# Row sums of a pairwise ranking on ScalarE, four buffers for the normalised rows and a loop over four batches

## The reference

```python
gt = xf.mean(axis=1) @ W_gt
kproj = xf @ W_k
score = jnp.einsum('bc,bnc->bn', gt, kproj) * SCALE
probs = jax.nn.softmax(score, axis=-1)
order = jnp.argsort(-probs, axis=-1)
reserve = order[:, :KEEP_NUM]          # KEEP_NUM = 1568 of 3136
...
```

## Time and profile before

| | us |
|---|---|
| median of 3 runs | 12256.19 (12219.48 to 12288.64) |
| profiled execution | 12231.48 |
| its span, first to last instruction | 12229.6 |
| VectorE busy | 9274.5 (76%) |
| TensorE busy | 8209.9 (67%) |
| ScalarE busy | 6990.4 (57%) |
| GpSimd busy | 2163.8 (18%) |

### The profile page before, as it was taken

How to read it: one execution, slowest core, us unless ns; L and a number is a source line. 1 busy time by engine, 2 the same in 40 slices (tenths; PEclk the granted TensorE clock), 3 DMA queues, 4 the chain that set the end, 5 groups by cost and what they waited for, 6 DMA issues and landing times. The chain is left out here.

```text
span 12229.6 us, 166452 instructions
## 1 busy us (share of the span) xinstructions
PE 8209.9 (67%) x45521; PEld 5308.0 (43%) x45521; DVE 9274.5 (76%) x26006; ACT 6990.4 (57%) x11527; POOL 2163.8 (18%) x1960
## 2 busy tenths in 40 slices
PE   4555577776575764767777677776576757344799
PEld 4555455554243432434444344443343434243587
DVE  8999544443898888989989889998889989655243
ACT  0000022112797975979999799997797979322222
POOL 2333211111000000000000000000000000077676
PEclk9999955555566655656666666665566666555555
DMA  3222100000000000000000000000000000143221
GB/s 90 71 76 63 31 22 19 20 19 21 11 17 12 18 11 12 16 12 17 17 15 18 14 14 18 18 14 14 15 14 14 18 12 15 29 96 85 54 58 40
DMA packets 669888, 351.94 MB, mean 29 GB/s; under 512 B 587281, under 2 KB 605680, under 8 KB 665056
## 3 DMA queue, kind: packets, MB, share of 16 engines
q1 hardware_dynamic: 607920, 242.84, 9.2%
q0 software_dynamic: 58624, 60.72, 1.9%
q10 hardware_dynamic: 2384, 37.11, 0.9%
HBM read 200.20 MB, written 147.72 MB: 28 GB/s over the span
## 5 line engine op out<-in xcount | busy, mean ns | idle before, releaser
L1040 PE MATMUL a_psT<-a_qt,a_kt 74*122 74x366 bf16 x3456 | 1556.8, 450 | 800.0 <-ACT a_pT L1120 558.5
L1270 DVE TENSOR_SCALAR_CACHE_REDUCE a_s<-a_psS 122x512 f32<-122x512 f32 (+1 forms) x2304 | 1605.3, 728 | 445.9 <-PE a_psS L1023 310.2
L1128 ACT ACTIVATE a_junk<-a_s,a_aim 122x1097 bf16<-122x1097 f32 x1152 | 1384.9, 1210 | 825.5 <-DVE a_s L1270 822.7
L1120 ACT ACTIVATE a_pT<-a_psT 122x732 f32<-122x732 f32 (+1 forms) x1920 | 1372.1, 715 | 598.3 <-PE a_psT L1043 594.4
L1204 DVE MAX8 a_near<-a_below 122x8 f32<-122x274 f32 (+1 forms) x4608 | 1699.3, 430 | 0.1
L1043 PEld LDWEIGHTS a_psT<-a_weigh,a_drops 122*122 122x122 bf16 x10368 | 1573.4, 191 | 193.0
L1197 DVE SCALAR_TENSOR_TENSOR a_below<-a_s,a_te,a_signs 122x1097 f32<-122x1097 f32 x1152 | 1546.4, 1352 | 128.7 <-remote 127.9
L1043 PE MATMUL a_psT<-a_weigh,a_drops 122*122 122x122 bf16 x10368 | 1527.9, 274 | 0.0
L1056 PE MATMUL a_psO<-a_pT,a_v 122*32 122x366 f32 x6912 | 1415.3, 704 | 0.0
L1128 ACT ACTIVATE a_signs<-a_s,a_te 122x1097 bf16<-122x1097 f32 x1152 | 1401.4, 1219 | 4.4 <-DVE a_te L1189 4.4
L1128 ACT ACTIVATE a_junk<-a_s,a_te 122x1097 bf16<-122x1097 f32 x1152 | 1385.1, 1205 | 0.0
(11 more groups left out here) (348 smaller groups left out, 14305.7 us busy)
## 6 DMA issues: line engine op xcount, KB each, us to landing
xbuf<-r_blank ACTq DMA_DIRECT2D x16, 1990.6 KB
e_xg<-xbuf SPq DMA_DIRECT2D x56, 568.8 KB
r_bc<-pr SPq DMA_DIRECT2D x16, 1372.0 KB, 7.4
a_k<-kT SPq DMA_DIRECT2D x384, 51.5 KB
a_q<-qT SPq DMA_DIRECT2D x384, 51.5 KB
a_kt<-kT SPq DMA_DIRECT2D x384, 51.5 KB
a_qt<-qT SPq DMA_DIRECT2D x384, 51.5 KB
r_xt<-in_x SPq DMA_DIRECT2D x16, 784.0 KB
```

The costliest lines, as they stand in the source:

```text
L1040: pe.matmul(out[:, x, 0:CW], kt[q][:, u * QP:(u + 1) * QP], qt[q][:, c * CW:(c + 1) * CW], start=True, stop=False)
L1120: act.activation(pT[j % RING][:, 0:w, :], psT[(q + j) % 2][:, 0:w, 0:CW], ACT.Exp).then_inc(exped, 1)
L1128: act.activation(out[:, :], s_[:, t, :], ACT.Sign, bias=at[:, t:t + 1], scale=-1.0, accum_out=total[:, t:t + 1]).then_inc(counted[r], 1)
L1270: dve.tensor_scalar(sc[o][:, t, a:b], psS[0:QP, a:b], 1.0, None, ALU.mult, ALU.max, accum_out=peaks[:, i, t:t + 1]).then_inc(evacuated, 1)
```

## The change

The row sums of rows 0 to 26 move to ScalarE. VectorE's comparison becomes a plain `tensor_scalar` without accumulator; ScalarE reads the bf16 marks, copies them into a throw-away tile `spill` and accumulates the row sum into the same `cnt[:, 1, j]`. A new semaphore `row_counted` frees the mark tiles together with `added`, so VectorE waits for both from row 4 on, and at the end of the batch for all 27. The last row keeps the old form. ScalarE's square and root for the next batch now stand between its copies, behind rows 1 and 6, and the clearing DMA at the start of the batch. `xls` and `idxs` get four buffers, the loop is written out for four batches per turn (four outside, a loop of two turns, four outside), and the parts move to later rows. Seventeen semaphores of `rank` are cleared at the start of `merge` on SyncE, ahead of its first loads.

```diff
-BEHIND = [0, 1, 8, 10, 11, 12, 13, 14, 15, 16]
+BEHIND = [0, 5, 10, 12, 13, 14, 15, 16, 17, 18]
+LAPS = 4
...
-        xls = [sb(f"r_xl{u}", [TP, NT, C + 1]) for u in range(2)]
+        xls = [sb(f"r_xl{u}", [TP, NT, C + 1]) for u in range(LAPS)]
...
-        idxs = [sb(f"r_idx{u}", [TP, NT], U32) for u in range(2)]
+        idxs = [sb(f"r_idx{u}", [TP, NT], U32) for u in range(LAPS)]
...
+        spill = [sb(f"r_spill{i}", [TP, N], BF16) for i in range(2)]
...
         def batches(eng, body):
 
-            for u in range(2):
-                body(0, u, True, u == 0 or B > 2)
-            if B > 4:
-                with eng.Fori(1, B // 2 - 1) as i:
-                    for u in range(2):
+            for u in range(LAPS):
+                body(0, u, True, True)
+            if B > 2 * LAPS:
+                with eng.Fori(1, B // LAPS - 1) as i:
+                    for u in range(LAPS):
                         body(i, u, False, True)
-            if B > 2:
-                for u in range(2):
-                    body(B // 2 - 1, u, False, u == 0)
+            for u in range(LAPS):
+                body(B // LAPS - 1, u, False, u < LAPS - 1)
 
...
-            with act.Fori(0, B) as b:
+
+            def square(b):
                 act.wait_ge(centred, b + 1)
                 act.activation(sq[:, :, :], xc[:, :, :], ACT.Square).then_inc(squared, 1)
+
+            def deviate(b):
                 act.wait_ge(varied, b + 1)
                 act.activation(sd, ve, ACT.Sqrt).then_inc(rooted, 1)
+
+            def body(i, u, first, more):
+                b = LAPS * i + u
                 act.dma_start(d.xbuf[bass.ds(b * TP * CLEAR, TP * CLEAR), :].rearrange("(p r) c -> p (r c)", p=TP),
                               blank[:, :, :].rearrange("p r c -> p (r c)")).then_inc(cleared, 16)
+                for j in range(NT - 1):
+                    act.wait_ge(compared, (NT - 1) * b + j + 1)
+                    if j >= 2 or not first or u:
+                        act.wait_ge(row_counted, (NT - 1) * b + j - 1)
+                    act.activation(spill[(u + j) % 2][:, j * TP:N], greater[j % MARKS][:, j * TP:N], ACT.Copy,
+                                   accum_out=cnt[:, 1, j:j + 1]).then_inc(row_counted, 1)
+                    if more and j == BEHIND[0] + 1:
+                        square(b + 1)
+                    if more and j == BEHIND[1] + 1:
+                        deviate(b + 1)
+
+            square(0)
+            deviate(0)
+            batches(act, body)
...
                 dve.wait_ge(prob_in, 16 * b + 16)
                 for j in range(NT):
                     at, to = j * TP, (j + 1) * TP
                     if j >= MARKS:
                         dve.wait_ge(added, (NT - 1) * b + j - MARKS + 1)
-
-                    more_ = dve.tensor_scalar(greater[j % MARKS][:, at:N], bc[:, at:N], rk[:, j:j + 1], None, ALU.is_gt,
-                                              ALU.add, accum_out=cnt[:, 1, j:j + 1])
+                        dve.wait_ge(row_counted, (NT - 1) * b + j - MARKS + 1)
+
                     if j < NT - 1:
-                        more_.then_inc(compared, 1)
+                        dve.tensor_scalar(greater[j % MARKS][:, at:N], bc[:, at:N], rk[:, j:j + 1], None,
+                                          ALU.is_gt).then_inc(compared, 1)
                     else:
-                        link.after(more_, 1)
+                        link.after(dve.tensor_scalar(greater[j % MARKS][:, at:N], bc[:, at:N], rk[:, j:j + 1], None, ALU.is_gt,
+                                                     ALU.add, accum_out=cnt[:, 1, j:j + 1]), 1)
                     link.after(dve.scalar_tensor_tensor(out=junk[j % 2][:, :], in0=bc[:, at:to], scalar=rk[:, j:j + 1],
                                                         in1=k.lower[:, :], op0=ALU.is_equal, op1=ALU.mult,
                                                         accum_out=cnt[:, 2, j:j + 1]), 1)
                     if more and j in BEHIND:
-                        if j == BEHIND[2] and not (first and u == 0):
-                            dve.wait_ge(scattered[1 - u], 16 * NT * (i + u))
-                            dve.wait_ge(laid[1 - u], 16 * (i + u))
-                        parts[BEHIND.index(j)](b + 1, 1 - u)
+                        v = (u + 1) % LAPS
+                        if j == BEHIND[2] and not (first and v):
+                            dve.wait_ge(scattered[v], 16 * NT * (i if v else i + 1))
+                            dve.wait_ge(laid[v], 16 * (i if v else i + 1))
+                        parts[BEHIND.index(j)](b + 1, v)
                 link.all()
                 dve.wait_ge(compared, (NT - 1) * (b + 1))
                 dve.wait_ge(added, (NT - 1) * (b + 1))
+                dve.wait_ge(row_counted, (NT - 1) * (b + 1))
...
+            for used in k.used:
+                sp.sem_clear(used)
             rows(0)
```

More of the change, by code:

```diff
@@ L229, in rank @@
          maxed, max_turned, max_one, max_all, sum_one, sum_all, probbed, prob_turned, prob_out,
-         prob_stored, prob_in, indexed, compared, added, taken, started, blanked, cleared) = (sem("r_" + x) for x in (
+         prob_stored, prob_in, indexed, compared, added, taken, started, blanked, cleared, row_counted) = (sem("r_" + x) for x in (
              "x_in", "centred", "squared", "varied", "rooted", "normed", "summed", "meaned", "gated",
@@ L233, in rank @@
              "probbed", "prob_turned", "prob_out", "prob_stored", "prob_in", "indexed",
-             "compared", "added", "taken", "started", "blanked", "cleared"))
-        scattered, laid = ([sem(f"r_{x}{u}") for u in range(2)] for x in ("scattered", "laid"))
+             "compared", "added", "taken", "started", "blanked", "cleared", "row_counted"))
+        scattered, laid = ([sem(f"r_{x}{u}") for u in range(LAPS)] for x in ("scattered", "laid"))
+        k.used = (*scattered, *laid, x_in, centred, squared, varied, rooted, normed, summed, meaned, gated, gtb_made)
         block = ctx.enter_context(nc.Block())
         def batches(eng, body):
-            for u in range(2):
-                body(0, u, True, u == 0 or B > 2)
-            if B > 4:
-                with eng.Fori(1, B // 2 - 1) as i:
-                    for u in range(2):
+            for u in range(LAPS):
[3 more added lines that the diff above has]
+                    for u in range(LAPS):
                         body(i, u, False, True)
-            if B > 2:
-                for u in range(2):
-                    body(B // 2 - 1, u, False, u == 0)
+            for u in range(LAPS):
+                body(B // LAPS - 1, u, False, u < LAPS - 1)
         def tokens(b):
@@ L267, in body @@
                 row = d.pr[bass.ds(b * NT, NT), :].rearrange("(a j) p -> a (j p)", a=1)
-                sp.dma_start(bcs[u][:, :], row.partition_broadcast(TP)).then_inc(prob_in, 16)
+                sp.dma_start(bcs[u % 2][:, :], row.partition_broadcast(TP)).then_inc(prob_in, 16)
                 sp.dma_start(d.y[bass.ds(b * N, N), :].rearrange("(j p) c -> p j c", p=TP), xls[u][:, :, 0:C]).then_inc(laid[u], 16)
             batches(sp, body)
-            for u in range(2):
-                sp.wait_ge(laid[u], 16 * (B // 2))
+            for u in range(LAPS):
+                sp.wait_ge(laid[u], 16 * (B // LAPS))
         @block.scalar
@@ L340, in body @@
                     if more and j in BEHIND[2:2 + len(parts)]:
-                        parts[BEHIND.index(j) - 2](b + 1, 1 - u)
+                        parts[BEHIND.index(j) - 2](b + 1, (u + 1) % LAPS)
             pe.wait_ge(started, 2)
@@ L356, in body @@
             def body(i, u, first, more):
-                pool.wait_ge(indexed, 2 * i + u + 1)
+                pool.wait_ge(indexed, LAPS * i + u + 1)
                 apart(pool, k)
@@ L364, in _ @@
             batches(pool, body)
-            for u in range(2):
-                pool.wait_ge(scattered[u], 16 * NT * (B // 2))
+            for u in range(LAPS):
+                pool.wait_ge(scattered[u], 16 * NT * (B // LAPS))
         @block.vector
@@ L444, in body @@
             def body(i, u, first, more):
-                b = 2 * i + u
-                bc, rk, idx = bcs[u], rks[u], idxs[u]
+                b = LAPS * i + u
+                bc, rk, idx = bcs[u % 2], rks[u % 2], idxs[u]
                 dve.wait_ge(prob_in, 16 * b + 16)
```

8 lines of the change are left out of this document (4 added, 4 removed).

## The result

The changed kernel takes 11967.17 us (median of 4 runs, 11962.35 to 11994.79) against 12248.78 us (4 runs, 12219.48 to 12288.64): ratio 0.9776, 95% interval 0.9759 to 0.9793. The prediction said 11,965. Its profiled execution has a span of 11960.6 us where the kernel before had 12229.6.

What follows compares the result with a forecast made beforehand. VectorE was taken to bound the ranking. Per batch 55.2 + 6.6 + 2.9 + 1.2 + 0.4 = 66.3 us (66.0 with overlap) gave 1042 against 1324.8, net -277 with end costs: forecast 11,965 us, range 11,900 to 12,040.

Steps and rivals of the forecast that it cites:

- What bounds the kernel: Ranking: VectorE sets the pace, busy 1216 of 1324.8 us; plain comparisons gain 23.2 us a batch.
- rival 1: Ranking comparisons: no fast reading, they keep their slope; only buffer and loop waits go, about 12,200 us; chance 4%.
- Row sums on ScalarE: Ranking: ScalarE needs 50.4 us a batch, no steady bound, but its lag makes VectorE wait 2.9 us a batch.
- rival 4: Ranking: ScalarE is the bound, with 0.7 us fixed per copy in place of 0.28; period 72, total 12,060 us; chance 8%.
- the walk: Row-by-row timing of a ranking batch with four tile buffers: VectorE waits 2.9 us, for rows 6, 7 and 8.
- two table loads of 1.28: ScalarE in each ranking batch: two loads of activation functions, 1.28 us each, within its 50.4 us.
- The parts, moved apart: Next batch's parts in the ranking: VectorE's waits for TensorE grow from 2.6 to 6.6 us a batch.
- The probabilities' way: Ranking: the probabilities' 8.9 us through memory to the broadcast is no longer fully hidden, costing 1.2 us a batch.
- Buffers and loop: Ranking: four buffers remove 25.1 us of scatter waits, fewer loop turns 12.8 us; clearing semaphores costs 1 us.
- The shared port: Ranking: fast comparisons hold GpSimd's scatters to 1.5 us in the mean, 50 us a batch; VectorE loses 0.4 us.
- rivals 2 and 3: GpSimd bounds the ranking from 2.06 us a scatter, about 12,120, 8%; or starves, slower over 2.8 us, about 12,750, 4%.
- rival 5: Ranking: TensorE's granted clock falls from 1.00 to half, bounding the period at 85; 12,240 us; chance 2%.

Runs made afterwards that it cites:

- replanning: Changed kernel with six mark tiles, VectorE's parts at other rows and TensorE's parts earlier in its queue: 11848.41 us, ratio 0.9676.
- old places: Changed kernel with the next batch's parts behind the rows that the kernel before had: 12003.21 us, ratio 0.9797.
- loop and buffers alone: Kernel before with only four buffers and the loop over four batches, sums still on VectorE: 12218.49 us, ratio 0.9976.
- control: Changed kernel without an edit, timed again beside three other kernels: 11953.10 us, ratio 0.9767.
- forms the sums twice: Changed kernel with VectorE's comparison accumulating again into an unread tile, ScalarE's copies kept: 12210.83 us, ratio 0.9966.

## Why the prediction was right, and where it was not

**What bounds the kernel; rival 1.** Right. The prediction read VectorE as the pace of the ranking; it lost 22.7 us of work a batch (363.1 / 16) where 23.2 were summed from the earlier trace rows. The plain form's slope held: 1.84 us from start to start at 2800 elements, in the batch that begins at 893, against 0.40 + 0.524 x 2.8 = 1.87. With the accumulator put back, 272 us returned, so the first rival (no fast reading) falls by an experiment and not by reading alone. The sum can be held against one batch, from 893.05, period 64.3: 0.66 us of waits at the tiles, 6.28 for TensorE's links (3.60, 1.82, 0.40, 0.46), 0.37 at the count's sum and 1.43 for the broadcast leave 55.6 for VectorE's own, as the sum had it (55.2 + 0.4). Three readings of the rows were loose: the durations of the earlier trace rows give 1.047 ns an element and not 1.042, 24 pairs in 2.37 us are 0.099 us each and not 0.096, and the 2.6 us of waits a batch count the first batch's 6.3 into the mean (2.25 without). None moves the sum by more than 0.4 us a batch.

**Row sums on ScalarE; rival 4.** The mechanism was right and two of its sizes were off. The wait costs 0.6 us a batch, not 2.9, and falls at row 10 (0.66 us ahead of the comparison at 917.95) where the walk had rows 6 to 8; the last batch alone waits 6.6. The fixed cost of a copy came out at 0.19 us from start to start (586.27 to 588.79 is 2.52 us at 2800 elements, of which 2.33 by 0.833 ns), where the prediction took 0.28 from an activation with pointer operands. "ScalarE: Activation LUTs" of the Trainium skill (§ What ACT_TABLE_LOAD costs) gives 186 ns for immediate operands; the trace agrees, with 2521 ns for a copy of 2800 elements, 189 ns over 0.833 ns an element. The larger miss is the term "two table loads of 1.28": I carried over as if a load belonged to the function, where it belongs to a change of functions as the program was built. The trace after has one load of each ahead of sixteen squares and roots, with copies between. Put back, the loads cost 22.8 us of the ranking's 27 us of error (period 64.2 and not 66.0, fifteen times), and the wait at the tiles is then 1.9 us a batch, where the walk had 2.3 with 0.19 us fixed. The same page of the Trainium skill (§ Table sets: the hidden batching unit) says that functions come in sets and that only a change of set costs; the trace after agrees, with 1 + 1 loads for 16 + 16 activations: behind the first root's load, fifteen squares, fifteen roots and all copies ran without another. The trace of before shows a program that paid although square and root can share one.

**The parts, moved apart.** Right to a few tenths: 3.6 us for the sums (predicted 3.7), 1.7 for the gate (2.0), 0.5 for the one behind (0.9 for two). Both experiments on the order took away what the prediction had named as its cause: the two rows of marks ahead of the gate (-45 us, the links behind the gate included), and the rows too few ahead of the sums (with the rest of the replanning and six tiles, -77).

**The probabilities' way.** 1.4 us a batch for 1.2, and 3.7 ahead of one batch, the one before the loop turns.

**Buffers and loop.** The buffers are necessary, which the prediction had missed: it credited them with 25.1 us, and with two of them the changed kernel is where the kernel before is (0.9982). The sum took the waits that they remove from today's periods; at the new pace a batch's scatters go on for some 50 us from its end (28 x 1.81), and the next normalisation is reached some 28 us after it (26.4 us behind the first comparison). The measured wait was 20.8; beside a VectorE that waits the 28 scatters took 46 to 48 us. At the loop's turn VectorE stood 5.6 us instead of 3.4. With the old places, where no broadcast is waited for, it stood 3.5, so the rest is perhaps the wait for the broadcast, put down to "issue", which no run shows. The 7.3 us put down to "issue" at line 502 belonged to the wait for the scatters, which fits the 48.5 us of loop and buffers alone. For the last scatters and the semaphores the sum had 6 us, and the gap behind the ranking grew by 4.3.

**The shared port; rivals 2 and 3.** Right, and the closest size of all: 1.506 us for 1.5, 50.6 us a batch. GpSimd still waits some 13 us a batch for the indices (of the 288.9 us, 104.6 stand ahead of the first scatter) and nobody waits for a scatter. The rivals needed 2.06 and 2.8 us. The point of rival 3 was whether GpSimd can take the port between two instructions that follow at once. The scatter of 579.73 did, at the end of the comparison: it was released 0.12 us behind it. The section "Who interferes with whom" of "SBUF — State Buffer" in the Trainium skill says that whoever comes second is fully blocked; this case agrees for the duration of one instruction, and its 1.506 us show that GpSimd doesn't starve beyond it.

**The clock; rival 5.** The granted clock stayed at 1.00 in the ranking's windows, TensorE busy 46 of 64 us.

**The sum.** The ranking is 305.7 us shorter where the sum had 277, and the spans differ by 269.0. The later stages gave back 36.7: 17.6 between and 19.1 at the end. The control gave back 22.7 between and took 3.1 at the end, so the end is accident; the some 20 us between stand in both executions of the changed kernel against one of the kernel before, and loop and buffers alone show as much (9262.0). By the medians the gain is 281.6 us, 24 less than the ranking's, and on the control's occasion 294.8, 12 less. That the median came within 2 us of the forecast is thus partly luck, two errors that cancelled: 29 us too little gain in the ranking, and 12 to 37 us lost behind it, in stages that I had called the same. The choice of 11,965 between 11,954 (profile) and 11,979 (median) did the rest.

## What to carry to other kernels

An accumulator on a compare can cost more than the sum: VectorE's plain form took half the time per element here, and an idle ScalarE formed the sums behind it. When one engine's work halves, walk the whole chain again, since links that hid behind it (TensorE's parts, the broadcast, the scatters' buffers) come out one by one, and their order was worth a further 73 us in the ranking. What a load of activation functions costs has to be counted from the order of the functions in the new program and not from the old trace.

## What the hardware showed unasked

- Sixteen squares and sixteen roots ran with one load of functions each when the copies were in the same stream, and with 16 + 16 loads of 1283 ns when they were not and stood in a loop by themselves. Which of the two, the copies or the form of the loop, does it was not tried apart.
- A turn of the loop stalls VectorE for 3.2 us in the kernel before (two batches in the body), 3.2 in the one with loop and buffers alone (four), 3.5 in the one with the old places (four), 5.6 in the changed kernel (four) and 10.0 in the one that forms the sums twice (four). These runs give no rule for the numbers.
- Stages whose code is the same took 9239 to 9273 us in fourteen executions of twelve kernels. The two kernels that were profiled twice repeated within 6 us, too few to tell a dependence on the kernel from accident.
